# Attention's head parities on separate row halves of the stacks, in a two-layer float32 kernel on one core

## What is computed

```python
def _L1_attn_ref(x, Wq, Wk, Wv, Wo):
    ...
    H, HKV = (32, 8)
    DH = E // H
    G = H // HKV
    ...
    qg = q.reshape(b, HKV, G, t, DH)
    scores = jnp.einsum('bhgtd,bhkd->bhgtk', qg.astype(jnp.float32), k.astype(jnp.float32)) / math.sqrt(DH)
    causal = jnp.tril(jnp.ones((t, t), dtype=bool))
    scores = jnp.where(causal[None, None, None], scores, jnp.finfo(jnp.float32).min)
    attn = jax.nn.softmax(scores, axis=-1).astype(x.dtype)
    ctx = jnp.einsum('bhgtk,bhkd->bhgtd', attn, v)
```

## Time and profile before

| | us |
|---|---|
| median of 3 runs | 1794.21 |
| lowest and highest run | 1789.66, 1794.48 |
| span of the profiled execution | 1792.7 |
| PE busy, of the span | 1521.2 (85%) |
| DVE busy | 1148.1 (64%) |
| ACT busy | 607.1 (34%) |
| POOL busy | 340.2 (19%) |

### The profile page before, as it was taken

One profiled execution on the slowest core, in us unless ns is written; L12 is line 12 of the kernel. 1 busy time (PEld: TensorE's weight loads), 2 busy tenths in 40 slices (PEclk: granted clock), 3 DMA queues, 4 the chain that ended last, 5 costly groups with the idle time before them and its releaser, 6 DMA issues. The chain is left out here.

```text
span 1792.7 us, 24031 instructions
## 1 busy us (share of the span) xinstructions
PE 1521.2 (85%) x7034; PEld 1036.6 (58%) x7034; DVE 1148.1 (64%) x2429; ACT 607.1 (34%) x859; POOL 340.2 (19%) x382
## 2 busy tenths in 40 slices
PE   0399889898846881999999999699999999999969
PEld 0366657566535660777777776355555555555447
DVE  5576875768645455455555543688687786888527
ACT  4224223242223330111111111046456465666632
POOL 2243343334312230000000000012122121121211
PEclk9988979889767895999999999579899898999979
DMA  7200000100023432100000000402112111211032
GB/s 263 94 1 1 24 24 1 47 1 24 1 89 125 150 124 89 30 25 18 24 25 18 15 9 0 87 8 48 28 27 54 27 27 27 54 27 29 2 131 82
DMA packets 48596, 84.12 MB, mean 47 GB/s; under 512 B 8899, under 2 KB 16657, under 8 KB 48506
## 3 DMA queue, kind: packets, MB, share of 16 engines
q1 hardware_dynamic: 41874, 78.13, 15.0%
q10 hardware_dynamic: 6632, 4.97, 0.9%
HBM read 58.54 MB, written 24.26 MB: 46 GB/s over the span
## 5 line engine op out<-in xcount | busy, mean ns | idle before, releaser
L1515 ACT ACTIVATE f_prob<-f_bank 128x1024 f32<-128x1024 f32 (+3 forms) x384 | 304.4, 811 | 216.6 <-PE f_bank L1612 214.5
L1594 PE MATMUL f_bank<-f_kst,f_qst 96*128 96x512 f32 (+3 forms) x768 | 282.8, 412 | 24.9 <-DMA f_qst<-q_scr 12.5
L1535 DVE CUSTOM_DVE_ANT_0 f_bank<-f_bank,f_mask 128x128 f32<-128x128 f32 (+3 forms) x512 | 248.5, 503 | 79.5 <-PE f_bank L1594 64.0
L1594 PEld LDWEIGHTS f_bank<-f_kst,f_qst 96*128 96x128 f32 x768 | 153.0, 204 | 181.0 <-DVE f_mx L1535 62.3
L1612 PE MATMUL f_bank<-f_qst,f_kst 98*128 98x512 f32 (+3 forms) x768 | 217.0, 367 | 1.2 <-ACT f_prob L1515 1.2
L1483 POOL TENSOR_SCALAR_AFFINE_SELECT f_prob<-f_prob 128x256 f32<-128x256 f32 x256 | 104.0, 407 | 467.8 <-ACT f_prob L1515 467.2
L1538 DVE TENSOR_REDUCE f_mx_first<-f_bank 128x1 f32<-128x512 f32 x256 | 176.1, 688 | 17.4 <-issue 8.1
L1630 PE MATMUL f_bank<-f_prob,f_vst 128*32 128x512 f32 (+3 forms) x1536 | 169.3, 514 | 1.0 <-ACT f_prob L1515 0.8
L37 PE MATMUL d_bank<-xtl,d_wgh 128*128 (+1 forms) x352 | 143.1, 407 | 8.9 <-DMA d_zz<-z_gu_scr 8.9
L1612 PEld LDWEIGHTS f_bank<-f_qst,f_kst 98*128 98x128 f32 x768 | 135.2, 199 | 20.6 <-ACT f_prob L1515 9.3
L1187 ACT ACTIVATE d_hs<-d_bank 128x512 f32<-128x512 f32 (+1 forms) x44 | 26.3, 598 | 348.8 <-PE d_bank L39 348.8
(11 more groups left out here) (225 smaller groups left out, 2761.6 us busy)
## 6 DMA issues: line engine op xcount, KB each, us to landing
f_qst<-q_scr SPq DMA_DIRECT2D x32, 384.0 KB, 6.1
q_scr<-c_qh SPq DMA_DIRECT2D x32, 256.0 KB
wst<-L_ffn_w SPq DMA_DIRECT2D x6, 1024.0 KB, 6.5
f_kst<-k_scr SPq DMA_DIRECT2D x32, 192.0 KB, 5.2
d_qw<-L_ffn_qweight_gu SPq DMA_DIRECT2D x40, 128.0 KB, 2.6
xall<-L_attn_x SPq DMA_DIRECT2D x2, 2048.0 KB, 16.2
xb<-L_attn_x SPq DMA_DIRECT2D x4, 1024.0 KB, 5.6
x_d<-xb SPq DMA_DIRECT2D x4, 1024.0 KB, 4.3
```

The lines of the kernel that those rows point to most:

```text
L1515: act.activation(prob[:, c // 2 % 2, c % 2 * 2:c % 2 * 2 + 2, lo:], score_bank[c % 2][:, :, lo:], ACT.Exp, scale=D ** -0.5).then_inc(exp_d ...
L1535: dve.tensor_tensor_reduce(sc, sc, mask[:, CH - w:CH], 1.0, LEAST, ALU.add, ALU.max, mx[:, u, h % 2, h // 2, q:q + 1]).then_inc(spare_free, 1)
L1594: pe.matmul(spare[v][:, 0:w], qst[0:M_ROW, u, h // 2, q * P:q * P + P], kst[0:M_ROW, u, h % 2, at:at + w], start=True, stop=True).then_inc ...
```

## The change

It does four things.

- Parity 1 moves from rows 48 to 95 to rows 64 to 111 of `qst` and `kst` (`stack_rows`). `kst` has one copy of the keys for both, the maxima lie in row 48 and row 112, and `fixed` has one column.
- `scores` issues its two matmuls over 49 rows each, the first from row 0, the second from row 64. `item` issues a matmul over 48 rows from row 0 or 64.
- `ITEMS` is ordered so that the two parities of the same query block and key stretch follow each other.
- An item of parity 0 waits for `spare_free` of `number + 2`: both its own bank and its partner's are free. One of parity 1 waits as before.

```diff
--- before.py
+++ after.py
@@ -1285,14 +1285,21 @@
 HALF = T // CH
 QPH = CH // P
 PART = 3 * D
-M_ROW = 2 * PART
+HALF_ROWS = P // 2
 STACKS = 3
 
 UNITS = [(0, k) for k in range(QPH)] + [(1, k) for k in (0, 4, 5, 6, 7, 1, 2, 3)]
 NU, NC = len(UNITS), 2 * len(UNITS)
 HEAD = 3
 
-ITEMS = [(h, q, at, min(CH, (q + 1) * P - at)) for h in range(HG) for q in range(QB) for at in range(0, (q + 1) * P, CH)]
+ITEMS = [(2 * i + par, q, at, min(CH, (q + 1) * P - at)) for i in range(HG // 2) for q in range(QB)
+         for at in range(0, (q + 1) * P, CH) for par in range(2)]
+
+
+def stack_rows(par, extra=0):
+
+    return slice(par * HALF_ROWS, par * HALF_ROWS + PART + extra)
+
 TURN_MAXIMA = 19
 TURN_FIRST_HALF = 10
 LOADED = 4 * 16
@@ -1343,9 +1350,9 @@
             return ctx.enter_context(nc.semaphore("f_" + name))
 
         ident, mask = sb("ident", [P, P]), sb("mask", [P, CH])
-        fixed = sb("fixed", [P, 2, 1])
-        qst = sb("qst", [P, STACKS, 2, T], F32R)
-        kst = sb("kst", [P, STACKS, 2, T], F32R)
+        fixed = sb("fixed", [P, 1])
+        qst = sb("qst", [P, STACKS, HG // 2, T], F32R)
+        kst = sb("kst", [P, STACKS, T], F32R)
         vst = sb("vst", [P, STACKS, QB, 2 * D])
         prob = sb("prob", [P, 2, HG, CH])
         mx = sb("mx", [P, STACKS, 2, 2, QB])
@@ -1434,8 +1441,8 @@
 
                 n, u, _ = g
                 for par in range(2):
-                    r = slice(par * PART, par * PART + PART)
-                    sp.dma_start(kst[r, u, par].bitcast(F32), k_scr[bass.ds(n, 1)].rearrange("n c d t -> (n c d) t")).then_inc(qk_in[u], 16)
+                    r = stack_rows(par)
+                    sp.dma_start(kst[r, u].bitcast(F32), k_scr[bass.ds(n, 1)].rearrange("n c d t -> (n c d) t")).then_inc(qk_in[u], 16)
                     src = q_scr[bass.ds(n * HG, HG)].rearrange("(i p) c d t -> p (c d) i t", p=2)[par]
                     sp.dma_start(qst[r, u].bitcast(F32), src).then_inc(qk_in[u], 16)
 
@@ -1445,7 +1452,8 @@
 
                 sp.wait_ge(spare_free, (NI if first else use_of(n - 1, "turn maxima")) + 1 + SPARE)
                 for par in range(2):
-                    sp.dma_start(qst[M_ROW + par:M_ROW + par + 1, u].rearrange("o i (b q) -> o (i b) q", q=P).bitcast(F32),
+                    row = par * HALF_ROWS + PART
+                    sp.dma_start(qst[row:row + 1, u].rearrange("o i (b q) -> o (i b) q", q=P).bitcast(F32),
                                  mt[par * 2 * QB:(par + 1) * 2 * QB, u].bitcast(F32)).then_inc(m_in[u], 16)
 
             def step(g, after, third):
@@ -1454,7 +1462,7 @@
                     sp.wait_ge(st_ps, g[0] * NC + NC)
                     load(third)
 
-            sp.dma_start(fixed[:, :, :], fixed_d).then_inc(fixed_in, 16)
+            sp.dma_start(fixed[:, :], fixed_d).then_inc(fixed_in, 16)
             for u in range(STACKS):
                 sp.wait_ge(cleared, u + 1)
                 load(group(0, u))
@@ -1520,7 +1528,7 @@
         def _(dve):
             dve.wait_ge(fixed_in, 16)
             for u in range(STACKS):
-                dve.tensor_copy(kst[:, u], fixed[:, :, :].broadcast_to([P, 2, T])).then_inc(cleared, 1)
+                dve.tensor_copy(kst[:, u], fixed[:, :].broadcast_to([P, T])).then_inc(cleared, 1)
             dve.sem_inc(spare_free, SPARE)
             dve.wait_ge(const_in, 32)
 
@@ -1590,9 +1598,10 @@
                 h, q, at, w = ITEMS[s]
                 if s == 0:
                     pe.wait_ge(qk_in[u], turns * LOADED + LOADED)
-                pe.wait_ge(spare_free, number + 1)
-                pe.matmul(spare[v][:, 0:w], qst[0:M_ROW, u, h // 2, q * P:q * P + P],
-                          kst[0:M_ROW, u, h % 2, at:at + w], start=True, stop=True).then_inc(spare_ps, 1)
+                pe.wait_ge(spare_free, number + (2 if h % 2 == 0 else 1))
+                r = stack_rows(h % 2)
+                pe.matmul(spare[v][:, 0:w], qst[r, u, h // 2, q * P:q * P + P], kst[r, u, at:at + w],
+                          start=True, stop=True).then_inc(spare_ps, 1)
 
             def maxima(g, number, v):
                 n, u, _ = g
@@ -1609,8 +1618,9 @@
                     pe.wait_ge(m_in[u], turns * (16 * 2) + 16 * 2)
                 pe.wait_ge(exp_done, n * NC + c + 1)
                 for hh in range(2):
-                    mm = pe.matmul(score_bank[c % 2][:, hh, lo:], kst[0:M_ROW + 2, u, hh, k * P:k * P + P],
-                                   qst[0:M_ROW + 2, u, c % 2, h * CH + lo:(h + 1) * CH], start=True, stop=True)
+                    r = stack_rows(hh, 1)
+                    mm = pe.matmul(score_bank[c % 2][:, hh, lo:], kst[r, u, k * P:k * P + P],
+                                   qst[r, u, c % 2, h * CH + lo:(h + 1) * CH], start=True, stop=True)
                 mm.then_inc(st_ps, 1)
 
             def weighed(g, i):
@@ -1881,8 +1891,8 @@
     mask[:, CH - P:] = np.triu(np.full((P, P), -1e30, f), 1)
     c["mask_d"] = mask
 
-    fixed = np.zeros((P, 2, 1), f)
-    fixed[M_ROW, 0], fixed[M_ROW + 1, 1] = -1, -1
+    fixed = np.zeros((P, 1), f)
+    fixed[PART], fixed[HALF_ROWS + PART] = -1, -1
     c["fixed_d"] = fixed
     return c
 
```

## The result

The changed kernel takes 1993.86 us (median of four runs, 1973.25 to 2011.62), the kernel before beside it 1791.93 us (1789.41 to 1794.48): the ratio is 1.1082, with a 95% interval of 1.1016 to 1.1147. The change costs 202 us, where 121 were forecast. The sign and the range hold; the time lies above the 1860 to 1980 given for the forecast's own case, on the way to the third rival (clock low nearly throughout, 2055).

A forecast was written before the change was run, and what follows sets the result against it. PE's streaming was taken to bound the wide steps. Waits +46, head +9, last groups -2 and clock +68 sum to +121 us on the profiled 1792.7, forecast 1915 us, range 1800 to 2050 for 8 in 10.

The forecast's parts named there:

- the forecast's own case: Whole kernel: waits as computed, clock low a fifth to seven tenths of the attention; 1860 to 1980 us, chance 0.32.
- the third rival: Attention: slower, clock low nearly throughout; +53 + 207, 2055 us, chance 0.15.
- PE bounds the wide steps by streaming: Attention's main part: PE is the bound; overlapping row halves cut its work from about 29 us a group to 23.
- The wait, +3.3 us a group, +46: Full-clock groups: even items wait for the item two before; 35.5 us against 32.2, over 14 groups +46 us.
- The head, +9: Maximum pass alone before the main part: pairs of items wait on DVE, 35.8 us against 26.2, less overlap, +9 us.
- The last two groups, -2: End of attention: overlapping scores pairs give about 3 us in the last group, the one before loses 1; -2 us.
- The clock, "I take 40%", +68: Attention groups: 40% of their time at half clock, from PE idling and half the rows at work; 93 - 25 = +68 us.
- Rival 1: Attention groups: faster, lags hidden and DVE becomes the bound at 28.3 us a group; -50, 1745 us, chance 0.19.
- the second rival: Attention: slower by the waits, with the clock as now; +53, 1847 us, chance 0.25.
- Rival 4: Scores and item pairs: halves don't overlap, a group takes 39.8 us; 1910 to 1950 us, chance 0.04.
- The signs named: Profile marks of being right: full-clock period 34 to 37 us, DVE idle 5 to 8, head 34 to 36, clock under 0.9.
- Scores pairs some ns apart: Scores on PE: the second matmul of a 512 pair starts some ns after the first, not 0.23 us.

## Why the prediction was right in sign and short in size

- **"PE bounds the wide steps by streaming", and overlap saves it.** Right, and small. Where 63 and 64 rows keep the clock up, the parts have prices of their own at full clock: row halves 32.2 to 30.7 us a group, the order back up to 31.1. Of the 6 us of PE work a group that the prediction counted as saved, 1.5 show in the time.
- **The wait, +3.3 us a group, +46.** The mechanism and the net were right. No whole group of the changed kernel stands at full clock, so that the named sign, a period of 34 to 37 us, can't be read directly. In the same kernel with 63 and 64 rows the fastest time of each of the twelve cycles, over 14 groups, sum to 35.9 us. That is an estimate: two of the twelve never stood at full clock, and the same sum is 0.4 under the true group in the kernel before. The prediction's working gave 35.9 and took 35.5. Against 32.2 that is 3.7 x 14 = +52. Inside it the wait alone is worth 5 us a group (35.9 against 31.1), the halves give back 1.5, and the order takes 0.4. The net agrees better than its parts. The order had no term of its own in the prediction; on full rows it is +24, on 48 and 49 rows it goes with at least 37 us less.
- **The head, +9.** It was +12. The step that failed is the count: 26.2 and 35.8 us were worked out for the 48 items of group 0, but the head also holds the dozen early items of group 1, the 60 or so of the windows row. 9.6 x 60 / 48 is 12.0.
- **The last two groups, -2.** With the wait and the low clock out of the way (63 and 64 rows, old wait) they take 58.5 us against 59.2 before, so -1; in the changed kernel 71.6, at a clock of 0.64.
- **The clock, "I take 40%", +68.** This is the step that failed. At 1.2 GHz were 73% of the main part, 527 of 722 us, which is the time of 10.3 cold groups of 51.3 us: 64% of the 16, where the sum had 40%. Of the span's 192 us, 12 are the head and 52 the wait's and order's at full clock; the other 128 are the clock, nearly twice the +68 (64% in the prediction's own sum would be 148 - 25 = +123). The price of a cold group was right (51.3 us, "about 50"); the share was not. The prediction named both idle time and rows at work as reasons and could not weigh them, and took a value nearer the lower bound since the blocks and turns keep their 128 rows. The runs weigh them: idle alone, on 96 and 98 rows, leaves 0.94; fewer rows alone give 0.54 to 0.60; 15 zero rows more bring 0.63 to 0.84; and with those rows the wait makes 0.84 of 0.92, so the two reasons add to each other. What the prediction read in the trace of before, that PE stayed at half clock in the head at 96 rows and rose after blocks of 128, is no proof for the rows: with 126 rows the head stays at half clock too.
- **Rival 1, DVE as the bound, 28.3 us a group.** Not reached. Even with neither wait nor clock loss the group stays at 30.7, with DVE busy 26.6.
- **Rivals 2 and 3.** The third is the nearer: its 2055 presumed a low clock nearly throughout, and it was low for 73% of the time. Had the clock stayed as before (the second rival), the forecast of 1847 would fit: 1792 + 12 + 52 is 1856.
- **Rival 4, no overlap.** Excluded by the timeline of PE and by the 31.1 and 30.7 us groups.
- **The signs named.** Clock under 0.9: yes. Scores pairs some ns apart: not as put; the scores matmul of the half that the item ahead leaves free starts some ns after that item, and its partner follows when its own half is free. DVE's idle time per group from 5 to 8: 8.9 in the kernel with the wait that holds its clock (37.6 - 28.7), 13 in the changed kernel's best group (41.4 - 28.3), as the low clock adds to it. Weight loads released by DVE most of the time: 212 of 380 us of idle time by the masked maxima alone. Head 34 to 36: 44.2, for the reason above.

## What to carry to other kernels

Before splitting matmuls onto parts of the array's rows, count the rows that each one covers: with fewer rows TensorE ran at half clock for 73% of this kernel's main part, the untouched matmuls too, though the profile shows it busy all the time. The other way round, where a matmul leaves rows unused and the granted clock dips, try zero rows up to 128; here they cost no time and gave 1%. And issue in pairs only with buffers for two pairs: with three banks a wait for two leaves the consumer one bank in hand, and producer and consumer take turns.

## What the runs showed of the hardware that was not expected

**Rows covered and the granted clock.** The same instructions in the main part, by rows of items and scores: 48 and 49 rows 0.54 to 0.65, 63 and 64 rows 0.84 to 0.92, 96 and 98 rows 0.94 to 0.95, 126 and 128 rows 0.98 to 0.99. With waits and order the same, the step from 48 to 63 rows is worth 0.21 to 0.35; the wait and the order move the clock by up to 0.11 on 48 rows, 0.08 on 63 and 0.01 on 96. The step from 63 to 96 is 0.03 to 0.10, no clearer than that spread, and the two differ in halves and full rows as well; the one from 96 to 126 is 0.03 to 0.04. What is shown is the step from 48 to 63 and, at the loop's turns, the one from 96 to 126. In the head the clock is 0.50 whatever the rows. Whether it is rows switched on or rows with data that count was not separated: zeros sufficed in these runs.

**A matmul may start ahead of an earlier one on the other half.** In the changed kernel at half clock:

```profile
1562.93 0.79 PE L1603 MATMUL f_bank<-f_kst,f_qst 48*128 48x512 f32 x1 [0.51 <-DVE f_mx L1543]
1563.02 1.13 PE L1622 MATMUL f_bank<-f_qst,f_kst 49*128 49x512 f32 x2
1563.61 0.62 PE L1603 MATMUL f_bank<-f_kst,f_qst 48*128 48x512 f32 x1
...
1564.19 1.02 ACT L1523 ACTIVATE f_prob<-f_bank 128x1024 f32<-128x1024 f32 x1 [0.82 <-PE f_bank L1622]
```

The even item starts at 1562.93 on rows 0 to 47. Of the scores pair, the matmul that starts at 1563.02 is the one that carries the announcement, the second in the program, on rows 64 on; the first, on rows 0 on, starts at 1563.52, behind the item on its own rows. ACT, released by that announcement, starts at 1564.19, after both. So each half is a stream of its own and takes the next matmul meant for it, and the announcement still came in order. In 185 of the 384 scores pairs of the changed kernel the matmul with the announcement starts first; in all 384 the announcement comes 13 to 23 ns after the later of the two ends as the profile gives them. The Trainium skill, page "TensorE: Matmul & The Clock Gate", section "The mechanism", says that matmuls start and end strictly in program order; these starts do not, while its conclusion, that one announcement on the last matmul is sound, is borne out.
